# Another order of all engines' work in an eight-batch fused kernel, with the first spread of a step behind the second convolution and its product behind the residual sum

## The reference

```python
x = x + conv_ref(_ln_c(x), ...)        # _ln_c: norm over the 64 channels of each pixel
#   conv_ref(v): g = groupnorm(v, 8 groups over channels and all pixels) * gn_w + gn_b
#                return v + w2 @ relu(w1 @ g + b1) + b2
t = to_tokens(x)                       # 16384 tokens a batch, 64 channels
t = t + ffn_ref(_ln_t(t), ...)         # _ln_t: norm over the channels of each token
#   ffn_ref(t): logits = t @ gate_w.T + gate_b        (32 experts)
#               probs = softmax(logits over groups of tokens)
#               the 8 best tokens of each expert are gathered, weighted and summed,
#               pass through the expert (gelu), and are scattered back, weighted
x = from_tokens(t)
```

## Time and profile before

| what | us |
|---|---|
| median of 3 runs | 654.55 |
| lowest and highest of the runs | 645.64, 656.82 |
| the profiled execution | 655.78 |
| its span in the trace | 653.7 |
| PE busy, DVE busy, ACT busy, POOL busy | 482.6, 472.0, 416.9, 271.9 |

### The profile page before, as it was taken

One profiled execution on the slowest core, in us unless ns is written; L12 is line 12 of the kernel. 1 busy time (PEld: TensorE's weight loads), 2 busy tenths in 40 slices (PEclk: granted clock), 3 DMA queues, 4 the chain that ended last, 5 costly groups with the idle time before them and its releaser, 6 DMA issues.

```text
span 653.7 us, 12854 instructions
## 1 busy us (share of the span) xinstructions
PE 482.6 (74%) x4964; PEld 198.7 (30%) x4964; DVE 472.0 (72%) x833; ACT 416.9 (64%) x635; POOL 271.9 (42%) x340
## 2 busy tenths in 40 slices
PE   5549898877878887897779787966778767578700
PEld 1213333332323323232323232322223222366600
DVE  6756776589769985996798669875887997974200
ACT  3547797669868985898688678872864466442000
POOL 1046340253036252626262526253553874220774
PEclk9769999989999999999999889987889898676855
DMA  7994578356746674568466746530114454100000
GB/s 261 389 413 134 191 213 276 118 179 231 253 128 220 216 242 133 202 243 233 152 226 194 230 135 217 197 130 32 65 66 130 134 144 137 37 5 2 11 13 9
DMA packets 36476, 106.86 MB, mean 163 GB/s; under 512 B 5176, under 2 KB 6200, under 8 KB 32320
## 3 DMA queue, kind: packets, MB, share of 16 engines
q1 hardware_dynamic: 34368, 105.00, 47.2%
q0 software_dynamic: 2048, 1.05, 0.9%
HBM read 71.95 MB, written 34.08 MB: 162 GB/s over the span
## 4 chain that ended last, share of the span: by engine, by line
DVE 37%; PE 32%; ACT 14%; issue 10%; POOL 5%; DMA 0%; DVEq 0%; ACTq 0%; POOLq 0%
PE st L438 10%; DVE us L1020 6%; PE cv L457 6%; DVE tok L1035 5%; PE tl L485 5%; POOL out_rows L1641 5%; DVE top_i L1118 5%; DVE xs L1028 5%; DVE cnd L1113 4%; ACT sqc L835 4%; ACT hid L819 4%; PE bc L561 3%; ACT junk L868 2%; DVE lg L1016 2%; PE cv L449 2%
## 5 line engine op out<-in xcount | busy, mean ns | idle before, releaser
L1535 POOL TENSOR_TENSOR xs<-xs,us 128x1024 f32<-128x1024 f32 x64 | 151.2, 2378 | 173.7 <-DVE gsum L1020 111.5
L1028 DVE SCALAR_TENSOR_TENSOR xs<-cv,vecs,xs 128x1024 f32<-128x1024 f32 x64 | 82.0, 1281 | 28.3 <-PE cv L457 28.1
L457 PE MATMUL cv<-hid,w2bd 64*64 64x512 f32 x512 | 71.0, 625 | 39.5 <-ACT hid L819 39.0
L849 ACT ACTIVATE sqx<-xs 128x1024 f32<-128x1024 f32 x64 | 67.1, 1049 | 35.8 <-PE st L438 35.0
L819 ACT ACTIVATE hid<-cv,b1n 128x1024 f32<-128x1024 f32 x64 | 70.7, 1105 | 24.0 <-PE cv L449 23.8
L1020 DVE CUSTOM_DVE_ANT_0 us<-us,bc 128x1024 f32<-128x1024 f32 x60 | 72.2, 1204 | 12.3 <-PE bc L561 11.1
L561 PE MATMUL bc<-rstd_s,spread 32*128 32x256 f32 x368 | 50.6, 354 | 41.3 <-DVE lg L1016 16.3
L449 PE MATMUL cv<-us,w1n 64*64 64x512 f32 x512 | 73.4, 645 | 9.2 <-DVE xs L1028 9.2
L1035 DVE STREAM_TRANSPOSE tok<-xs 128x1024 f32<-128x1024 f32 x64 | 79.4, 1241 | 0.8
L868 ACT ACTIVATE junk<-us 128x1024 bf16<-128x1024 f32 x64 | 67.4, 1053 | 17.5 <-DVE gsum L1020 16.7
L485 PE MATMUL tl<-xs,gcen 128*32 128x256 f32 x1024 | 74.4, 412 | 0.2
(11 more groups left out here) (244 smaller groups left out, 667.1 us busy)
## 6 DMA issues: line engine op xcount, KB each, us to landing
us<-in_raw SPq DMA_DIRECT2D x64, 512.0 KB, 4.4
xs<-in_x SPq DMA_DIRECT2D x32, 1024.0 KB, 5.1
out_rows<-tok SPq DMA_DIRECT2D x64, 512.0 KB, 3.5
us<-in_e_w SPq DMA_DIRECT2D x8, 260.0 KB
xs<-in_e_w SPq DMA_DIRECT2D x8, 256.0 KB
sqc<-out_rows,idx_all POOLq DMA_INDIRECT x32, 2.9
out_rows<-sqc,idx_all POOLq DMA_INDIRECT x32, 2.1
vecs<-in_b SPq DMA_DIRECT2D x4, 0.2 KB, 6.6
```

What stands on the lines that cost most here:

```text
L457: mm = pe.matmul(cv[C * h:C * h + C, CH * sl:CH * sl + CH], w2bd[r, r], hid[r, CH * h:CH * h + CH], start=True, stop=True)
L1028: nc.vector.scalar_tensor_tensor(out=xu, in0=cv[:], scalar=vecs[:, 3:4], in1=xu, op0=ALU.add, op1=ALU.add).then_inc(x1_done, 1)
L1535: nc.gpsimd.tensor_tensor(xu, xu, su, ALU.add).then_inc(s_done, 1)
```

## The change: another order

The work stays the same, instruction for instruction, but for a few waits. What changes is the order of the calls in `step` on PE, ACT and DVE and in POOL's loop, and the places in the tables. The main pieces:

- On PE `spread_at(it, (s, 0))` moves from between `conv1` and `conv2` to behind `conv2`; on DVE `use_at(it, (s, 0))` moves from ahead of `x1` to behind it.
- The S jobs begin at (3, 0) and not (3, 1), the fourth L job goes from (3, 0) to (7, 0), and the M job from (7, 0) to (0, 0) of the next pass.
- The search of a batch is spread over steps 3 to 7 and 0 and 1 of the next pass, where it took 3 to 7 and 0.
- The group norm of step 7: `norm_variance` goes from ahead of `x1` to behind `x1` and the fourth L product, and `norm_sums` waits for that product.
- `rstd` goes from the end of step 2 to ahead of its `x1`; the centring is one step earlier.
- On POOL three gathers are issued a pass earlier; the rest comes between the merges of the last pass.

```diff
-S_JOBS = {(3, 1): 0, (3, 2): 1, (4, 0): 2, (4, 1): 3, (5, 0): 4, (5, 1): 5, (6, 0): 6, (6, 1): 7}
-L_JOBS = {(1, 1): 0, (2, 0): 1, (2, 1): 2, (3, 0): 3}
+S_JOBS = {(3, 0): 0, (3, 1): 1, (4, 0): 2, (4, 1): 3, (5, 0): 4, (5, 1): 5, (6, 0): 6, (6, 1): 7}
+L_JOBS = {(1, 2): 0, (2, 0): 1, (2, 1): 2, (7, 0): 3}
...
             def norm_sums(it, n):
 
                 pe.wait_ge(gnred_ready, 2 * (n + 1))
+                if it >= 1:
+                    pe.wait_ge(bc_used, job_count(it, "L", 3))
...
             def step(it, s):
...
+                conv1(it, par, s)
                 if s == 0 and b >= 0:
                     x1_sums(b, b % 2, NG - 1)
-                conv1(it, par, s)
-                spread_at(it, (s, 0))
+                if s in (1, 2) and p2:
+                    xc_square_sums(n, s + 1)
                 centre(it, s)
...
                 conv2(it, s)
+                spread_at(it, (s, 0))
+                if s == NU - 1 and p1:
+                    norm_sums(it, n)
...
                 spread_at(it, (s, 1))
...
                 if b >= 0:
                     logits(b, b % 2, u)
+                if s in (3, 5, 7):
+                    x1_square_sums(it, (s - 3) // 2)
+                if s in (2, 4, 6):
+                    x1_sums(it, par, (s - 2) // 2)
...
+                if s in (5, 7) and p3:
+                    xc_square_sums(it + 2, (s - 5) // 2)
```

On DVE, in `step`:

```diff
-                if s < NU - 1 or not p1:
-                    use_at(it, (s, 0))
...
+                if s == 2 and p1 and it >= 1:
+                    rstd(n)
+                x1(it, par, s)
+                use_at(it, (s, 0))
...
+                if s == NU - 1 and p1:
                     norm_variance(n)
+                    norm_weights(n)
+                if s == NU - 1 and p1:
+                    norm_bias(n)
```

More of the change, by code:

```diff
@@ L640, in prologue @@
                     spread_stat(-1, "S", k)
-                norm_sums(0)
+                norm_sums(-1, 0)
                 norm_bias(0)
@@ L923, in step @@
                     norm_rsqrt(n)
-                if s == 2 and it == NB - 1:
-                    merge_exps(it - 2)
-                if s == 1 and 3 <= it < NB - 1:
-                    merge_exps(it - 3)
-                if s in (3, 7):
-                    centre_squares(it, s)
-                square_at(it, (s, 0))
+                if s >= 1 and square_later(it, s - 1):
+                    square_at(it, (s - 1, 1))
+                if s == 0 and late_piece(it):
+                    explog(it - 2, 2)
+                if s == 2 and late_piece(it):
+                    explog(it - 2, 3)
+                if s == 4 and t >= 0:
+                    explog(t, 0)
+                if not p1 and s in (5, 6):
+                    explog(t, s - 4)
+                square_at(it, (s, 0))
+                if s in SQUARES_AT:
+                    centre_squares(it, s, 0)
+                if s == 1 and 3 <= it:
+                    merge_exps(it - 3)
+                if s == 0 and b >= 0:
+                    ln2_mean_square(b)
+                if s == 5 and not p1:
+                    ln2_mean_square(NB - 1)
+                if s == NU - 1 and p1 and t >= 0:
+                    explog(t, 1)
+                if b >= 0:
+                    logits_copy(b, u)
+                if s == 0 and b >= 0:
+                    ln2_rsqrt(b)
+                if s in SQUARES_AT:
+                    centre_squares(it, s, 1)
                 if s >= 1:
@@ L1209, in step @@
                 b, u = (it, s - 1) if s else (it - 1, NU - 1)
-                values, places, _ = search_steps(it)
+                mid = p1 and t >= 0
                 if b >= 0:
@@ L1244, in step @@
                 use_at(it, (s, 2))
-                if it >= 2 and s == M_JOBS.get(it, (7, 0))[0]:
-                    find_best(it, it - 2)
-                if s == 2 and p1:
+                if s == 1 and late_piece(it):
+                    top_places(it - 2, 3)
+                if s == 2 and it == 0:
                     rstd(n)
-                if t >= 0 and s in values and s != NU - 1:
-                    top_values(t, values[s])
-                if t >= 0 and s in places and it + 2 == NB:
-                    top_places(t, places[s])
-                if s == 5 and not p1:
-                    ln2_variance(NB - 1)
-                if t >= POOL_MERGES and s == 6:
-                    candidates(t)
+                if mid and s in VALUES_AT and s != 5:
+                    top_values(t, VALUES_AT[s])
                 if not p1:
@@ L1259, in step @@
                         nc.vector.memset(ones[:], 1.0)
+                    if s == 3:
+                        top_values(t, 0)
                     if s == 4:
+                        top_values(t, 1)
+                        top_places(t, 1)
+                    if s == 5:
+                        top_values(t, 2)
+                        top_places(t, 2)
+                        top_values(t, 3)
+                        ln2_variance(NB - 1)
                         early_values()
```

167 lines of the change are left out of this document (63 added, 104 removed).

## The result

The changed kernel takes 767.77 us (median of 4 runs, 763.02 to 769.11), the kernel before 651.78 in the same session (645.64 to 656.82). The ratio is 1.180, with a 95% interval of 1.168 to 1.193. The profiled execution took 769.11 with a span of 766.9. The forecast was 718, its range 682 to 748: the sign was right, the size too small by 50 us.

What follows compares the result with a forecast made beforehand. No engine was full, so queue order and waits were taken to bound, with DVE bounding steps 3 to 6. Walked parts summed to +54.2 on 655.8, 710 us; clock dips added 8: 718 us, range 682 to 748.

Steps and rivals of the forecast that it cites:

- Term 1, the middle steps: Steps 2 to 6: the moved spread and product lengthen `x1` to `x1` to 8.3, 9.3, 8.3, 9.2 and 8.95 us.
- Term 2, the end of a pass: Step 7: ACT's work piles up behind `norm_rsqrt`, so `relu` of step 0 is late and the step costs 12.1 us.
- 9.1: Step 7: the least it can be, in us, if ACT's backlog lay beside something else.
- Term 3, steps 0 and 1: Steps 0 and 1, bounded by DVE: 7.9 and 7.2 us, with the 3.77 us wait for `rstd` gone.
- the M fold: Pass 6: the 7.67 us DVE wait for the fold of the M job goes, since that job is now early.
- Eight more dips at 1.0 us: +8: PE's clock: eight more lowered stretches behind gaps, at 1.0 us each, add 8 us to the walked time.
- the upper bound: PE's clock: 35 gaps at 1.2 us each, 42 us, giving 752 us.
- (a): Rival: PE's clock falls at most gaps, 25 to 35 dips at 1.2 us, 740 to 752 us; chance 0.18.
- (b): Rival: chains shorter than walked, in step 7 and steps 3, 5 and 6; about 672 to 690 us; chance 0.15.
- (c): Rival: faster, the waits removed outweigh the added chain if a middle step stays under 7.3 us; 625 us; chance 0.05.
- (d): Rival: no change, the faster rival and the longer end of the pass cancel; 645 to 668 us; chance 0.05.
- The signs named ahead: Expected profile: steps 4 and 5 at 8.3 and 9.2 us, PE gaps about 2.2, ACT's `gt` wait about 4.

Runs made afterwards that it cites:

- experiment 5: The changed kernel with the product put back ahead of `x1` on DVE, the first spread left behind `conv2`: 722.25 us, ratio 1.105.
- 6: The changed kernel with the first spread put back ahead of `conv2` on PE, the product left behind `x1`: 776.84 us, ratio 1.189.
- 13: The changed kernel with the product back ahead of `x1` and two unused matmuls ahead of each second spread: 693.21 us, ratio 1.060.
- 14: The changed kernel with the first spread back ahead of `conv2` and four unused matmuls ahead of each second spread: 730.52 us, ratio 1.116.
- experiment 1: The changed kernel with its gaps filled: four unused matmuls on PE ahead of the second spread in steps 0 to 6; 725.5 us, ratio 1.113.
- experiment 4: The changed kernel with ACT's centre square and `explog` of step 7 put ahead of `norm_rsqrt`: 766.1 us, ratio 1.176.
- experiment 12: The changed kernel with two unused matmuls ahead of each second spread: 728.82 us, ratio 1.117.
- experiment 8: The changed kernel, both moves undone, step 7's centre square and `explog` ahead of `norm_rsqrt`, four unused matmuls in step 2 of passes 1 to 6: 636.60 us.
- experiment 10: The kernel of experiment 8 plus four and five unused matmuls in step 2 of the last pass: 634.17 us, ratio 0.969.

## Why the prediction was wrong, point by point

- **Term 1, the middle steps: right.** Walked 8.3, 9.3, 8.3, 9.2, 8.95; with the gaps filled 8.24, 9.14, 8.31, 9.11, 8.84. That both moves make one cost, and not two, the prediction did not say; experiments 5, 6, 13 and 14 did. Its reading that DVE runs without a gap in steps 3 to 6 before, at 7.29 us, holds for steps 4 and 5 alone: in pass 4 steps 3 to 6 take 9.15, 7.29, 7.28 and 5.82. The sum goes by whole passes and is not touched by that.
- **Term 2, the end of a pass: right** (12.1, measured 12.03), with ACT's backlog as the walked cause. In the changed kernel the slow groups behind `norm_sums` left the step at 12.0 to 12.1; in experiment 1, where all three groups up to `conv1` were slow in most passes, PE was late for `conv2` and the step took 12.7 to 13.0. That 9.1 would be reached if it lay beside something else was too hopeful: experiment 4 came to 10.6 to 11.6, PE and the weights being late next.
- **Term 3, steps 0 and 1: right** (7.9 and 7.2; 7.78 and 7.34). The waits for `rstd`, in passes 2 to 6, and for the M fold went as said.
- **"Eight more dips at 1.0 us: +8" is the step that failed.** There were 35 gaps and slow groups behind 32, where before had 5; filling gave back 42.3 us, which is the upper bound that the prediction named and did not take. That the two agree so closely is in part luck, since the filled kernel still has slow groups, and part of the gain (2.5 us in step 0 of pass 0) lies at centring jobs that the 35 do not count. It chose eight by one argument, that a slow group fills the next gap. The rows show why this doesn't hold here: the gap is not left-over time that slower groups eat. It is set by `x1` and the product on DVE, which don't know of PE's clock, and so it is there in all five steps, 2.1 us long in four of them and about 4 or more in step 2. The earlier trace rows were the right rows, with one gap of 2.04 us and a fall; the earlier trace rows, the mean of 0.97, spoke for a pass that has one such gap and was taken to speak for one with five.
- **The rest, 15.6 us with the gaps filled,** is spread over all parts: in experiment 1, with its span of 723.5, pass 0 is 2.5 above the walked length, pass 1 3.4, passes 2 to 5 3.2, pass 6 2.8, pass 7 2.5, the tail 1.2. Each is small beside the clock, and part of it is clock too: step 7 of passes 1 to 5 and step 2 of passes 1 and 6, with their slow groups, are 6.7 us above the walk. In pass 0, step 2 (12.85 for 11.6), `conv1` stands behind a group of sums that waits 1.74 us for ACT's centre square, which the walk did not have.
- **The rivals.** (a), a fall at most gaps, was the right mechanism with 740 to 752; the missing 16 us are those of the point before. The Trainium skill ("TensorE: Matmul & The Clock Gate", "A second HAM failure mode: psum-queue depth-cycling") has it that short idle times between groups of matmuls make the clock swing, at a price in throughput. The trace agrees, with slow groups behind 32 gaps of 35. The 752 us that the prediction set beside that page was nearer than its forecast. (b), shorter chains, and (c) fell with the middle step, which with the gap filled takes 8.3 and not under 7.3. (d) fell.
- **The signs named ahead** were seen, but for the lengths of steps 4 and 5: gaps of 2.1 us with the product as releaser, DVE idle for 1.8 us or more ahead of `x1`, ACT's wait of 4.05 for `gt`, no wait ahead of `rstd` in passes 2 to 6, and pass 6 no longer the longest. In passes 1 to 5 step 4 took 8.3 us twice and 9.9 to 10.0 three times, step 5 9.1 once and 10.8 four times. Both had the walked length in all five passes once the gaps were filled.

## What to carry to other kernels

A call in an in-order queue costs what stands behind it: a spread and its product, each moved by one place, put the second spread and all behind it, `conv1` at the end, back by 1.8 us, since the queue of another engine tied them together, and the costs of two such moves don't add. When a change puts a gap into every step that another engine's work sets, price the clock at every gap, not at a few. A gap on PE that can't be closed may be worth filling: two or four matmuls of no use gave back 5% here, and 10 us in a kernel that already ran well.

## What the runs showed of the hardware

Behind gaps of 2.1 us and more ahead of a spread the matmuls of the changed kernel took up to twice their time for two or three groups, 32 times in 35: the granted clock came down from 2.4 to 1.2 GHz (0.50 in the window from 304 to 308 us, behind a gap of 4.06). Of the 27 gaps of 1.04 to 1.11 us that experiment 12 leaves in passes 0 to 6, 26 had only groups of full length behind them; of the 27 gaps of 1.32 to 1.44 us of experiment 5, 17 had a slow one. But the length of the last gap alone does not decide it. In experiment 1 four gaps of 2.13 and 2.14 us, in step 2 of passes 2 to 5, behind a filling, had groups of full length behind them, and in experiment 8 four gaps of 0.74 us did not. What else decides was not tested. I had not expected half of the filling to have nearly all of the effect (728.8 against 725.5 us), nor the fall to be so regular. It begins up to one group late: at 325.37 the logits still take 1.07, the sums at 326.25 take 1.71. And unused matmuls run at the clock that they find: in experiment 10 the four in the last pass took 3.78 us behind a `conv2` of 1.99, where four took 2.00 in experiment 1, so a filling that comes after the fall is itself slow.
